# Output bias of the experts: a one-hot product on TensorE, or a scaled row added by POOL

## The chip, the core and the metric

The kernel runs on one core of a Trainium2 chip. The metric is the time of one execution on the device, in microseconds (us), the median of several runs. The core's engines work side by side, each in the order of its own program, and meet at semaphores: TensorE (PE) multiplies matrices and writes PSUM, VectorE (DVE), ScalarE (ACT) and GpSimd (POOL) work on elements, SyncE (SP) starts loads and stores. DVE and ACT read PSUM and SBUF, POOL reads SBUF alone. POOL also issues the gathers and scatters by index.

## The reference

A decoder layer on four sequences of 512 tokens of 512 numbers, all in float32: self-attention, attention to a short memory, and a mixture of experts. The change is in the experts, of which the reference is:

```python
logits = h @ router_weight.T + router_bias
top_vals, top_idx = jax.lax.top_k(logits, TOP_K)          # 2 of 8
top_w = jax.nn.softmax(top_vals, axis=-1)
scores = jnp.zeros_like(logits).at[jnp.arange(T)[:, None], top_idx].set(top_w)
...
expert_out = jnp.einsum('eti,eih->eth', act, down_proj) + down_proj_bias[:, None, :]
out = jnp.einsum('te,eth->th', scores, expert_out)
```

Each token goes to two experts. An expert's output is `act @ down_proj` plus a bias row of that expert, `down_proj_bias[e]`, and the sum is multiplied by the token's share of that expert, `scores[t, e]`.

## The kernel before

**Stages.** The first 1055 us are the self-attention. From there to about 1175 the kernel attends to the memory, normalises, routes, and sorts the tokens by expert into tiles of 256 (`TILE`): 23 tiles (`NT`), the first eight for experts 0 to 7, the other fifteen given out by a table that is computed on the chip. From about 1175 to 1610 runs the expert loop, tile after tile; then the sums are copied to the output.

**One tile.** A tile `tau` has four units `u = 4 tau + ib`, one for each 128 of the 512 hidden numbers of the expert. A float32 product is made of three passes (`PASSES`): an operand is split into a high part, which ACT copies, and a low part, the rest, which DVE subtracts (`dve_lo`, L410). A unit goes round the engines like this:

- SP loads the unit's weights, `gu_raw` (512 KB, `sp_gu`, L1229) and `dn_raw` (256 KB, `sp_dn`, L1238), each into the place of the unit four before, once DVE has made the low part of that one. All these loads stand in one queue, in order.
- PE multiplies the gathered rows with the first weights (`pe_gu`, L1347: 24 products, two units ahead of the rest) into a PSUM bank.
- DVE makes `gate` and `up` of it (L1381, L1383: one input in PSUM, a bias column), then `gu_lo` for three units later (L410), then, after ACT's `sig`, the products `sig` and `up` (L1388, L1390), `dn_lo` and `act_lo` (L410).
- ACT makes `sig` (L1402), `gu_hi` for four units later, `act_hi` and `dn_hi` for the next unit (L306).
- PE multiplies `act` with the second weights (`pe_dn`, L1368: three products of 128x512 for each half tile of 128 tokens), adding up over the four units in one PSUM bank per half tile.

**Once per tile.** At the end of unit 3 PE transposes the rows of the tile after the next (`pe_rows`, L1318); ACT and DVE split them in unit 2 of the tile that follows (`act_rows`, `dve_rows`), and DVE takes the tokens' shares of the expert from the gathered rows (`dve_shares`, L1300 and L1304: `sh`, one number per token). In unit 1 of the next tile ACT reads the finished bank of each half, multiplies it with `sh` and writes `y`, which lies in `ctx_raw` (`act_y`, L1420; semaphore `ys_done`). POOL waits for both halves and for the landing of the scatters before, and then issues two scatters that add `y` to the sums in memory (`pool_y`, L1266). Behind these on POOL stand the two gathers of rows for three tiles later (`pool_rows`, L1254).

**The bias before.** The eight bias rows are loaded once (L1438) into `down_raw`, which POOL has filled with zeros (L1608); ACT and DVE split them into a high part in partitions 0 to 7 and a low part in 32 to 39 of `down_bias` (L1521, L1581). `expert_hot` has a column per tile, 1 in the two partitions of the tile's expert (L977, L1178, from `expert_row`). The first product of each half tile's bank is this column, spread over 128 tokens, with `down_bias` (L1366, 128x512); the other products add to it. So the bias is in the bank when ACT scales it.

**Order.** Each engine's order is the program's, at the end of `decoder_layer` (L1424 to L1642). On ACT a unit is `sig`, `gu_hi`, `act_hi`, `dn_hi`, then what comes once per tile. On SP a step is `sp_gu(u)`, `sp_dn(u - 3)`. On POOL a step is `pool_rows(tau + 2)`, `pool_y(tau)`.

Of the kernel before, what the change touches and what calls it, by code (L numbers as in the profile page):

```python
# [15 lines left out]
F32 = mybir.dt.float32  # L16
F32R = mybir.dt.float32r
# [82 lines left out]
def decoder_layer(nc, x, ctx, ctx_cols, mem_mask, wqkv, wo_rows, router_cols, router_b, gu_w, gu_b, down_w, down_b,  # L100
                  cos_t, sin_t, causal_t, ident_t, iota_t, out):
    stack = ExitStack()
    with stack:
# [701 lines left out]
        empty = st("empty", [P, 2 * NT])  # L805
        expert_row = st("expert_row", [P, 1])
        before_me = st("before_me", [P, P], BF16)
# [28 lines left out]
        bias_add = st("bias_add", [P, IB, 2])  # L836
        down_raw = st("down_raw", [P, D])
        down_bias = st("down_bias", [P, D], F32R)
        expert_hot = st("expert_hot", [P, NT], F32R)
        idx = st("idx", [P, 2 * NT], U32)  # L840
# [11 lines left out]
        for pre in ("m_", "h_"):  # L852
# [5 lines left out]
                   "const_done", "diff_done", "gexp_done", "gate_step", "sel_done", "share_done",  # L858
                   "rank_mm", "down_in", "down_hi", "down_lo", "row_done", "lane_done", "slots_mm", "slots_done", "hot_first", "hot_done", "idx_mm", "empty_done", "idx_done", "place_done", "pos_done", "h_in0", "h_in1", "h_in2", "h_in3", "share_in", "acc_in",
                   "count_mm", "table", "table_done",  # L860
# [3 lines left out]
                   "ah_done", "al_done", "dn_mm", "y_first", "ys_done", "y_add", "out_done"]  # L864
        CONSTS = 16
        z = {name: sem("z_" + name) for name in names2}
# [88 lines left out]
        def pe_idx_first(pe):  # L955

            pe.wait_ge(z["hot_first"], 3)
            pe.wait_ge(z["slots_done"], 1)
            nc.tensor.matmul(SLOTS[:, IDX_AT:IDX_AT + 2 * E], slots[:, :], row_hot[:, 0:2 * E], start=True, stop=True).then_inc(z["idx_mm"], 1)

        def pe_idx_rest(pe):

            pe.wait_ge(z["hot_done"], 2)
            nc.tensor.matmul(LATE_IDX[:, 0:2 * NX], slots[:, :], row_hot[:, 2 * E:2 * NT], start=True, stop=True).then_inc(z["idx_mm"], 1)
# [5 lines left out]
        def dve_first_tiles(dve):  # L970

            dve.wait_ge(z["const_done"], CONSTS - 1)
            nc.vector.tensor_tensor(tile_hot[:, 0:E, :], e_iota[:, :].unsqueeze(1).to_broadcast([P, E, E + 1]),
                                    t_iota[:, 0:E].unsqueeze(2).to_broadcast([P, E, E + 1]), ALU.is_equal).then_inc(z["hot_first"], 1)
            nc.vector.tensor_scalar(row_hot[:, 0:2 * E], first_row[:, :, :].rearrange("p e h -> p (e h)"), row_iota[:, 0:1], None,
                                    ALU.is_equal).then_inc(z["hot_first"], 1)
            nc.vector.tensor_scalar(expert_hot[:, 0:E], t_iota[:, 0:E], expert_row[:, 0:1], None, ALU.is_equal).then_inc(z["hot_first"], 1)  # L977

# [161 lines left out]
        def dve_table(dve):  # L1140
# [6 lines left out]
            def then(ins):  # L1147
# [29 lines left out]
                                    ALU.is_equal).then_inc(z["hot_done"], 1)  # L1177
            nc.vector.tensor_scalar(expert_hot[:, E:NT], tile_e[:, :], expert_row[:, 0:1], None, ALU.is_equal).then_inc(z["hot_done"], 1)  # L1178

# [172 lines left out]
        def pe_dn(pe, u):  # L1352
# [4 lines left out]
            pe.wait_ge(z["dn_lo_done"], u + 1)  # L1357
            if u == 0:
                pe.wait_ge(z["down_lo"], 1)
            for h in range(2):  # L1360
                n = 2 * tau + h
                if ib == 0:
                    if n == 2:
                        pe.wait_ge(z["idx_done"], 2)
                    wait(pe, z["ys_done"], n - 2)
                    nc.tensor.matmul(Y_BANK[n % 3][:, :], expert_hot[:, tau:tau + 1].to_broadcast([P, P]), down_bias[:, :], start=True, stop=False)  # L1366
                for sp_, mp in PASSES:
                    last = nc.tensor.matmul(Y_BANK[n % 3][:, :], act_st[sp_][:, w, h * P:(h + 1) * P], dn[mp][:, ib, :],  # L1368
                                            start=False, stop=(ib == IB - 1 and (sp_, mp) == PASSES[-1]))
                if h == 0 and ib == IB - 1:  # L1370
# [33 lines left out]
        def act_hi(act, u):  # L1404
# [3 lines left out]
            act_split(act_st[0][:, w, :], up[:, w, :], z["ah_done"])  # L1408

        def act_y(act, tau):  # L1410

# [12 lines left out]
        with nc.Block() as block:  # L1424

            @block.sync
            def _(sp):
# [7 lines left out]
                sp.dma_start(iota[:, :], iota_t).then_inc(z["small_in"], 16)  # L1435
                sp.wait_ge(z["const_done"], 1)
                for at in (0, 32):
                    sp.dma_start(down_raw[at:at + E, :], down_b).then_inc(z["down_in"], 16)  # L1438

# [64 lines left out]
            def _(act):  # L1504
                for k in range(ROUNDS):
# [11 lines left out]
                    if k == TOP_AT + IB + 1:  # L1517
                        act_dn_hi(act, 0)
                    if k == H_AT:
                        act.wait_ge(z["down_in"], 32)  # L1520
                        act_split(down_bias[:, :], down_raw[:, :], z["down_hi"])  # L1521
                act_slots(act)
                act_rows(act, 0)
                for u in range(NU):
# [9 lines left out]
                    if ib == 1 and tau:  # L1534
                        act_y(act, tau - 1)
                act_y(act, NT - 1)

            @block.vector
            def _(dve):
                for k in range(ROUNDS):  # L1540
# [37 lines left out]
                    on(lambda t: dve_m_inv(dve, t), k, EXP_AT)  # L1578
                    if k == TOP_AT:
                        dve.wait_ge(z["down_hi"], 1)  # L1580
                        nc.vector.tensor_tensor(down_bias[32:2 * 32, :], down_raw[32:2 * 32, :], down_bias[32:2 * 32, :].bitcast(F32),  # L1581
                                                ALU.subtract).then_inc(z["down_lo"], 1)
# [4 lines left out]
                dve.wait_ge(z["hot_first"], 3)  # L1587
                dve_shares(dve, 0)
# [18 lines left out]
            def _(pool):  # L1607
                nc.gpsimd.memset(down_raw[:, :], 0.0).then_inc(z["const_done"], 1)  # L1608
                for view, steps, base, by_row in ((tok_id[:, :], [[P, TT]], 1, 1), (e_start[:, :], [[T, E + 1]], 0, 0), (e_rows[:, :], [[T // P, E + 1]], TILE // P, 0),
                                                   (first_row[:, :, :], [[T // P, E], [1, TILE // P]], 0, 0),  # L1610
                                                   (e_iota[:, :], [[1, E + 1]], 0, 0), (t_iota[:, :], [[1, NT]], 0, 0), (k_tile[:, :], [[TILE, E - 1]], TILE, 0),
                                                   (row_iota[:, :], [[0, 1]], 0, 1), (lane_iota[:, :], [[1, P]], 0, 0),
                                                   (empty_id[:, :, :], [[0, NT], [P, 2]], T + 1, 1), (expert_row[:, :], [[0, 1]], 0, 1)):
                    nc.gpsimd.iota(view, steps, base=base, channel_multiplier=by_row,
                                   allow_small_or_imprecise_dtypes=True).then_inc(z["const_done"], 1)
                pool.wait_ge(z["const_done"], 12)
                nc.gpsimd.tensor_scalar(expert_row[32:2 * 32, :], expert_row[32:2 * 32, :], -32.0, None, ALU.add).then_inc(z["const_done"], 1)
                pool.wait_ge(z["const_done"], 13)
                nc.gpsimd.memset(ones[:, :], 1.0).then_inc(z["const_done"], 1)
                pool.wait_ge(z["const_done"], 14)  # L1620
                nc.gpsimd.affine_select(before_me[:, :], ones[:, :], [[1, P]], ALU.is_gt, 0.0, base=0, channel_multiplier=-1).then_inc(z["const_done"], 1)
# [76 lines left out]
```

## Time and profile before

| | us |
|---|---|
| median of 3 runs | 1630.09 (1629.74 to 1633.28) |
| the profiled execution | 1634.84 |
| its span, first to last instruction | 1633.0 |
| PE busy | 1489.3 (91%) |
| DVE busy | 1374.6 (84%) |
| ACT busy | 1057.3 (65%) |
| POOL busy | 841.3 (52%) |

The profile is of one execution, which took a little longer than the median. Busy times are sums over stages of different kinds. Matmuls overlap each other, so a full PE isn't PE at its peak rate. A view of the profile names an operation by its line and its output and input tiles; a helper's line (L306 for ACT's copies, L410 for DVE's low parts) stands for many steps, which the tile names tell apart.

### The profile page before, as it was taken

The numbers are of one execution on the slowest core, as the hardware profiler recorded it, in microseconds if no ns is written. First come the engines' busy times: TensorE is split into PE (matmuls) and PEld (weight loads), VectorE is DVE, ScalarE is ACT, GpSimd is POOL, SyncE is SP. The second block draws the span as 40 slices with busy tenths as digits, with TensorE's granted clock in tenths as the row PEclk, the third lists the DMA queues.
The fourth block names the chain that finished last, engine by engine and source line by source line (L and its number), as shares of the span: only waits on it lengthen the run. The fifth ranks groups of instructions, "written<-read, shape, count | busy, mean of one in ns | idle before, by whom it ended". The sixth has DMA issues, their size and how long they took to land. (4 is left out here: it accounts for less than half of the span.)

```text
span 1633.0 us, 31154 instructions
## 1 busy us (share of the span) xinstructions
PE 1489.3 (91%) x8952; PEld 1313.6 (80%) x8952; DVE 1374.6 (84%) x3583; ACT 1057.3 (65%) x2464; POOL 841.3 (52%) x1024
## 2 busy tenths in 40 slices
PE   5789999999999899999999999688699999999994
PEld 4678888888888778888878878578589999999993
DVE  7788898898898788889889889578689988998892
ACT  3677777777777677777777777343146666666661
POOL 7657657657657466656656755267312223222321
PEclk9799999999999999999999999966599999999997
DMA  4000000000000000000000000141458778877775
GB/s 175 1 14 20 2 14 21 1 14 21 1 14 20 3 14 20 1 15 21 1 15 1 1 1 1 32 146 74 142 146 243 234 228 221 225 228 218 198 178 135
DMA packets 62030, 124.95 MB, mean 77 GB/s; under 512 B 20942, under 2 KB 21070, under 8 KB 61792
## 3 DMA queue, kind: packets, MB, share of 16 engines
q1 hardware_dynamic: 51408, 102.24, 19.5%
q0 software_dynamic: 10304, 20.59, 6.5%
q8 instruction: 77, 1.26, 0.3%
q14 instruction: 97, 0.79, 0.2%
q10 hardware_dynamic: 144, 0.07, 0.0%
HBM read 106.08 MB, written 24.71 MB: 80 GB/s over the span
## 5 line engine op out<-in xcount | busy, mean ns | idle before, releaser
L313 ACT ACTIVATE probs<-probs,neg_max 128x512 f32<-128x512 f32 (+3 forms) x512 | 281.7, 552 | 46.4 <-DVE neg_max L422 44.1
L546 POOL TENSOR_SCALAR probs<-probs,row_inv 128x512 f32<-128x512 f32 (+3 forms) x512 | 263.8, 534 | 42.8 <-DVE row_inv L429 42.8
L537 POOL TENSOR_TENSOR rot<-rot,sin 128x512 f32<-128x512 f32 (+1 forms) x96 | 123.8, 1289 | 308.0 <-DVE rot L441 303.7
L218 PE MATMUL bank<-ident,probs 128*128 128x128 f32 x1280 | 186.0, 276 | 59.6 <-DVE pt_lo L410 50.0
L410 DVE TENSOR_TENSOR pt_lo<-bank,pt_hi 128x512 fp32r<-128x512 f32 (+1 forms) x384 | 216.2, 590 | 26.5 <-ACT pt_hi L306 26.4
L306 ACT ACTIVATE pt_hi<-bank 128x512 fp32r<-128x512 f32 (+1 forms) x384 | 186.2, 518 | 74.3 <-PE bank L218 66.2
L422 DVE CUSTOM_DVE_ANT_0 probs<-bank,causal 128x512 f32<-128x512 f32 (+3 forms) x512 | 219.6, 481 | 10.9 <-issue 3.6
L1266 POOL DMA_INDIRECT acc<-ctx_raw,idx x46 | 75.5, 1642 | 297.2 <-ACT ctx_raw L1420 283.0
L218 PEld LDWEIGHTS bank<-ident,probs 128*128 128x128 f32 x1280 | 151.1, 142 | 94.9 <-DVE pt_lo L410 54.7
L1347 PE MATMUL bank<-xt_hi,gu_hi 128*128 128x256 f32 x736 | 209.0, 284 | 3.5 <-issue 2.0
L1347 PE MATMUL bank<-xt_hi,gu_lo 128*128 128x256 f32 x736 | 207.2, 282 | 0.0
L1347 PE MATMUL bank<-xt_lo,gu_hi 128*128 128x256 f32 x736 | 207.2, 281 | 0.0
L208 PE MATMUL bank<-k_hi,q_st 128*128 128x256 f32 (+2 forms) x512 | 173.0, 349 | 2.5 <-DVE xn_lo L410 2.5
L235 PE MATMUL bank<-pt_hi,v_st 128*128 128x256 f32 (+2 forms) x512 | 172.5, 348 | 1.6 <-DVE pt_lo L410 1.6
L208 PE MATMUL bank<-k_lo,q_st 128*128 128x256 f32 (+2 forms) x512 | 157.4, 329 | 0.0
L235 PE MATMUL bank<-pt_lo,v_st 128*128 128x256 f32 (+2 forms) x512 | 156.8, 328 | 0.0
L185 PE MATMUL bank<-xn_hi,w_hi 128*128 128x512 f32 x384 | 153.6, 400 | 0.2 <-DVE rot L441 0.2
L185 PE MATMUL bank<-xn_lo,w_hi 128*128 128x512 f32 x384 | 151.9, 396 | 0.0
L185 PE MATMUL bank<-xn_hi,w_lo 128*128 128x512 f32 x384 | 151.6, 395 | 0.0
L1347 PEld LDWEIGHTS bank<-xt_hi,gu_hi 128*128 128x128 f32 x736 | 139.9, 190 | 7.5 <-issue 4.2
L1347 PEld LDWEIGHTS bank<-xt_lo,gu_hi 128*128 128x128 f32 x736 | 140.2, 190 | 3.0
L1347 PEld LDWEIGHTS bank<-xt_hi,gu_lo 128*128 128x128 f32 x736 | 139.9, 190 | 0.0
(204 smaller groups left out, 3915.0 us busy)
## 6 DMA issues: line engine op xcount, KB each, us to landing
gu_raw<-in_gate_up SPq DMA_DIRECT2D x92, 512.0 KB, 4.3
dn_raw<-in_down SPq DMA_DIRECT2D x92, 256.0 KB, 3.7
w_raw<-in_wqkv SPq DMA_DIRECT2D x8, 768.0 KB, 4.2
w_raw<-in_wo_rows SPq DMA_DIRECT2D x8, 512.0 KB, 3.5
h_rows<-ln_h SPq DMA_DIRECT2D x16, 256.0 KB, 2.0
acc<-x_res SPq DMA_DIRECT2D x4, 1024.0 KB, 5.0
x_res<-in_x SPq DMA_DIRECT2D x3, 1024.0 KB, 11.1
ctx_raw<-in_ctx SPq DMA_DIRECT2D x2, 512.0 KB, 6.9
```

The costliest lines, as they stand in the source:

```text
L185: last = nc.tensor.matmul(PJ_BANK[:, :], w1[sp][:, c, r * P:(r + 1) * P], xn[mp][:, c, b * L:(b + 1) * L], start=first, stop=(c == DC - 1 ...
L208: last = nc.tensor.matmul(S_BANK[k][:, at:at + cols], q_st[:, h, i * P:(i + 1) * P], kk[:, kb, 0:cols], start=(a == 0), stop=(a == 1))
L218: last = nc.tensor.transpose(T_BANK[u % 2][:, k * P:(k + 1) * P], probs[:, hb, P_AT[i] + j * P:P_AT[i] + (j + 1) * P], ident[:, :])
L235: last = nc.tensor.matmul(dst, v_st[:, vb, j, :], rhs, start=(j == 0 and a == 0), stop=(j == QB - 1 and a == 1))
L306: nc.scalar.activation(dst, src, ACT.Copy).then_inc(sem_, 1)
L313: nc.scalar.activation(row, row, ACT.Exp, bias=neg_max[:, hb, i:i + 1], scale=-1.0, accum_out=row_sum[:, hb, i:i + 1]).then_inc(s["exp_don ...
L410: nc.vector.tensor_tensor(dst, src, hi.bitcast(F32), ALU.subtract).then_inc(sem_, 1)
L422: nc.vector.tensor_tensor_reduce(out=probs[:, hb, P_AT[i]:P_AT[i] + (i + 1) * P], in0=S_BANK[k][:, at:at + (i + 1) * P], in1=causal[:, (QB ...
L537: nc.gpsimd.tensor_tensor(rot[0:rows, :], rot[0:rows, :], sin[0:rows, :], ALU.mult).then_inc(s["rot_sin"], 1)
L546: nc.gpsimd.tensor_scalar(row, row, row_inv[:, hb, i:i + 1], 0.0, ALU.mult, ALU.add).then_inc(s["pnorm_done"], 1)
L1266: nc.gpsimd.indirect_dma_start(out=acc, out_offset=bass.IndirectOffsetOnAxis(ap=idx[:, 2 * tau + h:2 * tau + h + 1], axis=0), in_=y[:, 2 * ...
L1347: last = nc.tensor.matmul(GU_BANK[u % 3][:, side * TILE:(side + 1) * TILE], gu[sp_][:, ib, c, side, :], xts[mp][:, k, c, :], start=first, ...
```

## The change

The one-hot product goes, and with it `expert_row`, `expert_hot`, `down_raw`, the split of the bias and the fill with zeros. The first of the other products now starts each bank. Per tile SP loads the expert's bias row to all 128 partitions (256 KB, two buffers), behind the tile's first `dn_raw`. ACT multiplies it with `sh` for each half tile into `y_b` (`act_bias`), behind the last unit's `dn_hi`. POOL adds `y_b` to `y`, one sum of 128x512 for each half as soon as ACT has written it, and waits for both sums ahead of its scatters. The wait of DVE for the use of `sh` three tiles before now asks for POOL's sums instead of ACT's `y`.

```diff
         def sp_dn(sp, e, u):
-            ib = u % IB
+            tau, ib = divmod(u, IB)
             wait(sp, z["dn_lo_done"], u - IB + 1)
             sp.dma_start(dn_raw[:, ib, :], down_w.rearrange("e i h -> (e i) h")[bass.ds(e * I + ib * P, P), :]).then_inc(z[f"dn_in{ib}"], 16)
+            if ib == 0:
+                wait(sp, z["b_scaled"], 2 * (tau - 1))
+                sp.dma_start(down_bias[:, tau % 2, :], down_b[bass.ds(e, 1), :].partition_broadcast(P)).then_inc(z[f"d_in{tau % 2}"], 16)
...
         def pool_y(pool, tau):
...
-            pool.wait_ge(z["ys_done"], 2 * tau + 2)
+            for h in range(2):
+                pool.wait_ge(z["ys_done"], 2 * tau + h + 1)
+                pool.wait_ge(z["b_scaled"], 2 * tau + h + 1)
+                nc.gpsimd.tensor_tensor(y[:, 2 * k + h, :], y[:, 2 * k + h, :], y_b[:, 2 * k + h, :], ALU.add).then_inc(z["y_bias"], 1)
+            pool.wait_ge(z["y_bias"], 2 * tau + 2)
             wait(pool, z["y_add"], 32 * tau)
...
         def dve_shares(dve, tau):
...
-            wait(dve, z["ys_done"], 2 * (tau - 2))
+            wait(dve, z["y_bias"], 2 * (tau - 2))
...
         def pe_dn(pe, u):
...
-            if u == 0:
-                pe.wait_ge(z["down_lo"], 1)
...
                     wait(pe, z["ys_done"], n - 2)
-                    nc.tensor.matmul(Y_BANK[n % 3][:, :], expert_hot[:, tau:tau + 1].to_broadcast([P, P]), down_bias[:, :], start=True, stop=False)
                 for sp_, mp in PASSES:
                     last = nc.tensor.matmul(Y_BANK[n % 3][:, :], act_st[sp_][:, w, h * P:(h + 1) * P], dn[mp][:, ib, :],
-                                            start=False, stop=(ib == IB - 1 and (sp_, mp) == PASSES[-1]))
+                                            start=(ib == 0 and (sp_, mp) == PASSES[0]), stop=(ib == IB - 1 and (sp_, mp) == PASSES[-1]))
...
+        def act_bias(act, tau):
+
+            k = tau % 2
+            act.wait_ge(z["sh_done"], tau + 1)
+            act.wait_ge(z[f"d_in{k}"], 16 * (tau // 2 + 1))
+            wait(act, z["y_bias"], 2 * (tau - 1))
+            for h in range(2):
+                nc.scalar.activation(y_b[:, 2 * k + h, :], down_bias[:, k, :], ACT.Copy, scale=sh[:, tau % 3, h:h + 1]).then_inc(z["b_scaled"], 1)
...
                     if ib == 1 and tau:
                         act_y(act, tau - 1)
+                    if ib == 3:
+                        act_bias(act, tau)
...
-                nc.gpsimd.memset(down_raw[:, :], 0.0).then_inc(z["const_done"], 1)
```

Left out are the other lines of the old bias (L977, L1178, L1436 to L1438, L1519 to L1521, L1579 to L1582, L1617), the new buffers `down_bias` (two rows) and `y_b` (four half tiles), and the counts of the semaphores that follow from them.

## Rows read from the trace of the kernel before

**Rows 1.** Windows of 18 us: busy time by engine, granted clock, DMA share, GB/s

```profile
core 0: us, PE busy (x) PEld busy (x) DVE busy (x) ACT busy (x) POOL busy (x), PEclk, DMA share, GB/s
1403.00:1421.00 18.00, 18.00 (x131) 16.75 (x130) 16.12 (x34) 11.39 (x20) 5.14 (x4) 1.00 0.85 235
```

**Rows 2.** Chain that ended last, from 1140 on by line, and pieces: start, us, what

```profile
by line: PE bank L1347 49.9%; PE bank L1368 24.0%; PE bank L1318 4.3%; issue 2.9%; PE bank L1366 2.0%; POOL at_lane L1130 1.3%; DMA acc<-ctx_raw,idx 1.0%; DVE gu_lo L410 0.9%; PE bank L951 0.8%; DMA xg<-h_rows,idx 0.7%; POOL acc L1266 0.6%;
...
1195.54 0.50 PE bank L1366
...
1214.96 0.87 PE bank L1318 x8
...
1218.65 0.23 PE bank L1366
...
1579.20 0.87 PE bank L1318 x8
```

**Rows 3.** Waits from 1240 to 1560: engine, for whom, us, times, longest

```profile
DVE gate L1381 <- PE bank L1347: 20.2, 17, 1.2
```

**Rows 4.** Timeline of ACT: start, us, line, operation, [idle before, and for whom]

```profile
1417.34 0.62 ACT L306 ACTIVATE dn_hi<-dn_raw 128x512 fp32r<-128x512 f32 x1
1417.86 1.25 ACT L1420 ACTIVATE ctx_raw<-bank,sh 128x512 f32<-128x512 f32 x2
...
1427.97 0.62 ACT L306 ACTIVATE dn_hi<-dn_raw 128x512 fp32r<-128x512 f32 x1
1429.18 0.42 ACT L1402 ACTIVATE sig<-gate 128x256 f32<-128x256 f32 x1 [0.59 <-DVE gate L1381]
```

**Rows 5.** Timeline of DVE in the same tile

```profile
1417.50 0.42 DVE L410 TENSOR_TENSOR act_lo<-up,act_hi 128x256 fp32r<-128x256 f32 x1
1419.04 0.48 DVE L1381 TENSOR_SCALAR gate<-bank,bias 128x256 f32<-128x256 f32 x1 [1.13 <-PE bank L1347]
1419.44 0.47 DVE L1383 TENSOR_SCALAR up<-bank,bias 128x256 f32<-128x256 f32 x1
1419.84 1.22 DVE L410 TENSOR_TENSOR gu_lo<-gu_raw,gu_hi 128x1024 fp32r<-128x1024 f32 x1
1420.97 0.42 DVE L1388 TENSOR_TENSOR sig<-sig,gate 128x256 f32<-128x256 f32 x1
```

**Rows 6.** DMA issues: operation, count, KB each, median us to landing

```profile
gu_raw<-in_gate_up SPq DMA_DIRECT2D x92, 512.0 KB, 4.3
...
xg<-h_rows,idx POOLq DMA_INDIRECT x46, 5.1
```

**Rows 7.** Timelines of POOL and DVE, where both have two SBUF inputs; lines (ns min/median/max)

```profile
1134.16 1.27 POOL L1222 TENSOR_TENSOR gu_lo<-gu_raw,gu_hi 128x512 fp32r<-128x512 f32 x1
...
1134.31 1.15 DVE L1085 TENSOR_TENSOR g_w<-g_w,g_exp 128x4 f32<-128x4 f32 x1
...
L1085 DVE TENSOR_TENSOR g_w<-g_w,g_exp x4: 145/158/1146, 1107.9 to 1167.4; 128x4 f32<-128x4 f32 x4
...
43.76 1.62 POOL L539 TENSOR_TENSOR rope<-rope,rot 128x512 f32<-128x512 f32 x1
...
43.58 0.68 DVE L447 TENSOR_TENSOR q_st<-rope,q_st 64x512 fp32r<-64x512 f32 x1
44.27 1.66 DVE L448 TENSOR_TENSOR q_st<-rope,q_st 64x512 fp32r<-64x512 f32 x1
...
L448 DVE TENSOR_TENSOR q_st<-rope,q_st x64: 685/687/1655, 44.3 to 1016.6; 64x512 fp32r<-64x512 f32 x64
...
L475 DVE TENSOR_TENSOR o_f<-bank,v_and_o x128: 669/683/685, 73.6 to 1046.2; 64x512 f32<-64x512 f32 x128
```

**Rows 8.** Timeline of POOL in the tile of rows 4 and 5

```profile
1419.57 1.63 POOL L1266 DMA_INDIRECT acc<-ctx_raw,idx  x1 [12.01 <-ACT ctx_raw L1420]
...
1424.98 1.04 POOL L1254 DMA_INDIRECT xg<-h_rows,idx  x1 [0.30 <-issue]
```

**Rows 9.** Chain that ended last, in the routing stage

```profile
1086.37 0.68 DVE down_bias L1581
```

**Rows 10.** Timelines of ACT and POOL at the end of the expert loop

```profile
1608.95 1.30 ACT L1420 ACTIVATE ctx_raw<-bank,sh 128x512 f32<-128x512 f32 x2 [1.64 <-PE bank L1368]
...
1611.27 1.57 POOL L1266 DMA_INDIRECT acc<-ctx_raw,idx  x1 [3.87 <-DMA acc<-ctx_raw,idx]
```

More of the change, by code:

```diff
@@ L805, in decoder_layer @@
         empty = st("empty", [P, 2 * NT])
-        expert_row = st("expert_row", [P, 1])
         before_me = st("before_me", [P, P], BF16)
@@ L836, in decoder_layer @@
         bias_add = st("bias_add", [P, IB, 2])
-        down_raw = st("down_raw", [P, D])
-        down_bias = st("down_bias", [P, D], F32R)
-        expert_hot = st("expert_hot", [P, NT], F32R)
+        down_bias = st("down_bias", [P, 2, D])
+        y_b = st("y_b", [P, 4, D])
         idx = st("idx", [P, 2 * NT], U32)
@@ L858, in decoder_layer @@
                    "const_done", "diff_done", "gexp_done", "gate_step", "sel_done", "share_done",
-                   "rank_mm", "down_in", "down_hi", "down_lo", "row_done", "lane_done", "slots_mm", "slots_done", "hot_first", "hot_done", "idx_mm", "empty_done", "idx_done", "place_done", "pos_done", "h_in0", "h_in1", "h_in2", "h_in3", "share_in", "acc_in",
+                   "rank_mm", "d_in0", "d_in1", "b_scaled", "y_bias", "row_done", "lane_done", "slots_mm", "slots_done", "hot_first", "hot_done", "idx_mm", "empty_done", "idx_done", "place_done", "pos_done", "h_in0", "h_in1", "h_in2", "h_in3", "share_in", "acc_in",
                    "count_mm", "table", "table_done",
@@ L864, in decoder_layer @@
                    "ah_done", "al_done", "dn_mm", "y_first", "ys_done", "y_add", "out_done"]
-        CONSTS = 16
+        CONSTS = 13
         z = {name: sem("z_" + name) for name in names2}
@@ L955, in pe_idx_first @@
         def pe_idx_first(pe):
-            pe.wait_ge(z["hot_first"], 3)
+            pe.wait_ge(z["hot_first"], 2)
             pe.wait_ge(z["slots_done"], 1)
@@ L961, in pe_idx_rest @@
         def pe_idx_rest(pe):
-            pe.wait_ge(z["hot_done"], 2)
+            pe.wait_ge(z["hot_done"], 1)
             nc.tensor.matmul(LATE_IDX[:, 0:2 * NX], slots[:, :], row_hot[:, 2 * E:2 * NT], start=True, stop=True).then_inc(z["idx_mm"], 1)
@@ L1177, in dve_table @@
                                     ALU.is_equal).then_inc(z["hot_done"], 1)
-            nc.vector.tensor_scalar(expert_hot[:, E:NT], tile_e[:, :], expert_row[:, 0:1], None, ALU.is_equal).then_inc(z["hot_done"], 1)
         def dve_at(dve, t):
@@ L1435, in _ @@
                 sp.dma_start(iota[:, :], iota_t).then_inc(z["small_in"], 16)
-                sp.wait_ge(z["const_done"], 1)
-                for at in (0, 32):
-                    sp.dma_start(down_raw[at:at + E, :], down_b).then_inc(z["down_in"], 16)
                 for u in range(IB):
@@ L1518, in _ @@
                         act_dn_hi(act, 0)
-                    if k == H_AT:
-                        act.wait_ge(z["down_in"], 32)
-                        act_split(down_bias[:, :], down_raw[:, :], z["down_hi"])
                 act_slots(act)
@@ L1578, in _ @@
                     on(lambda t: dve_m_inv(dve, t), k, EXP_AT)
[L1579 to L1582, printed above, removed]
                 dve_idx(dve, 1, 0, 2 * E, SLOTS[:, IDX_AT:IDX_AT + 2 * E])
@@ L1586, in _ @@
                 dve_rows(dve, 0)
-                dve.wait_ge(z["hot_first"], 3)
+                dve.wait_ge(z["hot_first"], 2)
                 dve_shares(dve, 0)
@@ L1612, in _ @@
                                                    (row_iota[:, :], [[0, 1]], 0, 1), (lane_iota[:, :], [[1, P]], 0, 0),
-                                                   (empty_id[:, :, :], [[0, NT], [P, 2]], T + 1, 1), (expert_row[:, :], [[0, 1]], 0, 1)):
+                                                   (empty_id[:, :, :], [[0, NT], [P, 2]], T + 1, 1)):
                     nc.gpsimd.iota(view, steps, base=base, channel_multiplier=by_row,
                                    allow_small_or_imprecise_dtypes=True).then_inc(z["const_done"], 1)
-                pool.wait_ge(z["const_done"], 12)
-                nc.gpsimd.tensor_scalar(expert_row[32:2 * 32, :], expert_row[32:2 * 32, :], -32.0, None, ALU.add).then_inc(z["const_done"], 1)
-                pool.wait_ge(z["const_done"], 13)
                 nc.gpsimd.memset(ones[:, :], 1.0).then_inc(z["const_done"], 1)
-                pool.wait_ge(z["const_done"], 14)
+                pool.wait_ge(z["const_done"], 11)
                 nc.gpsimd.affine_select(before_me[:, :], ones[:, :], [[1, P]], ALU.is_gt, 0.0, base=0, channel_multiplier=-1).then_inc(z["const_done"], 1)
```

1 line of the change is left out of this document (removed).

## The prediction

> **What bounds the kernel now.** I read the windows first, then the chain that ended last, then the waits, then one tile engine by engine. In the windows of the expert loop TensorE is busy for all of its 18.00 us at a granted clock of 1.00, and VectorE (DVE) for 16.12 of them [rows 1]: one engine is full and the next is close behind. The chain says the same: from 1214.96 to 1579.20 it is TensorE alone, 20 tiles apart, so a tile takes 364.24 / 20 = 18.21 us [rows 2]. How close DVE is, the waits tell: in 320 us of this loop its `gate` step waited 17 times for TensorE, 20.2 us together [rows 3], 1.19 us per tile. Left alone, DVE would need 18.21 - 1.19 = 17.02 us per tile. So taking work from TensorE can win at most 1.19 us per tile before DVE becomes the pace, and anything that holds DVE up by more than that loses.
>
> **The change, part by part.**
>
> TensorE loses two one-hot products per tile. On the chain one takes 0.23 us (the first 0.50), and all of them are 2.0% of its 493 us, 9.9 us [rows 2]. TensorE's tile falls to 18.21 - 0.47 = 17.74 us.
>
> ACT gains two scalings of 128x512 per tile, behind the `dn_hi` copy of the last quarter, ahead of the next `sig`. A copy of that shape took 0.62 us [rows 4]. They start near 1428.5 and end near 1429.7, so `sig`, at 1429.18, moves by some 0.5 us. DVE doesn't want it until its `gu_lo` is over: from the start of `gate` to that of the `sig` product are 1.93 us (1419.04 to 1420.97) [rows 5], of which `gate` and `sig` themselves need 0.48 + 0.42, so 1.03 are spare. Cost: 0. Without that cover, 0.5 us per tile, 11 in all. The scalings wait for a bias that SyncE asked for more than a tile earlier and for POOL's sums of two tiles before, and DVE's `sh` step for those of three before: all long done.
>
> SyncE gains one 256 KB load per tile, between two weight loads; queued behind it, and behind its wait for the scalings of two tiles before, are all later weights. That wait is over when its turn comes: the `dn_lo` that SyncE waits for just ahead of it follows, on DVE, a `sig` that ACT runs behind those scalings. A 512 KB load lands after a median 4.3 us [rows 6], and a bias is used 1.75 tiles after its turn comes. In bytes it is 0.25 MB on top of about 4.2 MB per tile (235 GB/s for 18 us), at a DMA share of 0.85 [rows 1]: some 0.05 more. Reading one row 128 times isn't in the trace; between 0 and one more 512 KB load, 4.3 us, it stays inside its cover. I take 0.
>
> POOL gains two sums of 128x512 per tile, and these I expect to decide. Three questions: what one costs, whom it stops, and where it falls.
>
> One costs 1.27 us: that is what POOL took for a two-input operation of this shape [rows 7].
>
> Whom it stops is shown by two places of the trace [rows 7]. At 1134.16 POOL begins such an operation; DVE's `g_w`, 4 elements from two SBUF inputs, begins 0.15 later and takes 1.15 us, where the shortest took 0.145. It was held for 1.00 us, to 1.15 us after POOL began. At 43.58 DVE runs `q_st` (two SBUF inputs) and POOL's operation takes 1.62: it waited 0.35 us for DVE, got in ahead of DVE's next operation, and that took 1.66 where 0.685 is normal, so DVE was let in at 45.24, 1.13 us after POOL at 44.11. So each waits for the other's whole operation, by turns, 1.13 to 1.15 us for DVE per sum. DVE operations with one input in PSUM don't take part: 128 of `o_f`, spread over the stage in which `q_st` was held so, took 0.669 to 0.685 us [rows 7]. In the expert loop `gate` and `up` read PSUM; `gu_lo`, the two products, `dn_lo` and `act_lo` have both inputs in SBUF.
>
> The Trainium skill (SBUF — State Buffer, "Who interferes with whom") has this as an exclusive lock held for the full instruction, the second one blocked until the first finishes. By it a sum would stop DVE for its full 1.27 us, where the rows give 1.13; the sum below would be 21 x 2 x 0.14 = 5.9 us higher.
>
> Where it falls: take the tile at 1417.50 [rows 4, 5]. If DVE did not wait for TensorE, `gate` would follow `act_lo` at 1417.84 (operations in a row overlap by 0.08, as `gate` and `up` do), `up` at 1418.24, `gu_lo` at 1418.64. ACT writes the first half tile of y from 1417.86 to about 1418.53 and the second to 1419.11. The first sum starts at 1418.53 at the earliest, and at the latest 0.46 later, the lag of today's scatter behind y [rows 4, 8]. If it is ahead of `gu_lo`, it holds that to about 1419.74, 1.10 late; `gu_lo` takes 1.13; the second sum then goes ahead of the `sig` product and holds it 1.13. Together 2.2 us. If `gu_lo` is first, the first sum holds the `sig` product for 1.13 and the second the next product for about 1.0: 2.1 us. Bounds: 0, if both sums fall where DVE reads PSUM or stands, and 2 x 1.27 = 2.54. I take 2.2, since no idle time of DVE is left to hide them once it is the pace.
>
> DVE's tile is then 17.02 + 2.2 = 19.22 us against TensorE's 17.74: DVE paces, and a tile takes 1.01 us more than 18.21. Sums fall in tiles 1 to 22; in the last, DVE has other gaps. 21 x 1.01 = +21.2 us.
>
> What is queued behind the sums on POOL: today's two scatters and then two gathers. Scatters start at 1419.57, the last gather is issued at 1424.98 and lands 5.1 us later [rows 6, 8], near 1430.1; TensorE transposes these rows at 1214.96 + 12 x 18.21 = 1433.5. With the sums the scatter starts near 1422.0 + 0.1 + 0.46 = 1422.6, 3.0 later, and the slack of 3.4 is nearly used up, in a tile that is 1.0 longer. A gather late by less than about 1 us makes `gate` wait just where the first sum would have held DVE, so it adds nothing. Cost 0; more under the rivals.
>
> The start: the fill, an index step and a shift on POOL, two small loads, a split on ACT and three small steps on DVE go. Only DVE's `down_bias`, 0.68 us, lies on the chain [rows 9]; the rest ends ahead of something that waits for a load or for TensorE. Between 0 and -0.7; I take -0.7, because the chain goes right through it.
>
> The end: y's last half is ready at 1608.95 + 1.30 = 1610.25, and its scatter starts at 1611.27, held by the landing of the scatter before [rows 10]. With two sums, 1609.6 + 2 x 1.27 + 0.46 = 1612.6 at the least, +1.4; by way of the scatter before, later by its own two sums less the 0.6 that the first half is ready sooner, +2.0. I take +1.8.
>
> Sum: 21.2 - 0.7 + 1.8 = +22.3 us against the profiled execution's 1634.84 us (span 1633.0). That one is 4.75 above the median of 1630.09; I add the difference to the median: **1652 us**.
>
> **Rivals.**
> *Faster, TensorE stays the pace.* It takes DVE being held less than 17.74 - 17.02 = 0.72 us per tile by the two sums in the stretch from `gate` to the second product. For it: 0.8 us of `gate` and `up` read PSUM, and today's 1.19 us wait stands right there, so the first sum could pass almost unseen, and perhaps the second between two short operations. Against it: the sums are 2.5 us together and follow each other at once, and the free stretch, today some 2 us, shrinks as TensorE gets faster. Price: -9.9 - 0.7 + 1.8 = -8.8, 1621 us. The sign turns at about 1.14 us per tile (21 x (1.14 - 1.19) = -1.1).
> *One sum collides, the other doesn't.* DVE is held 1.13: its tile is 18.15, -0.06 x 21 - 0.7 + 1.8 = about 0: 1630 us. For and against as above.
> *The port is held to POOL's recorded end, or the gather is late as well.* The first gives +5.9: 1658 us; a mechanism of this kernel's two sums, against which the two rows of 1.13 and 1.15 speak. For the second, a gather that lands 3 us later than the median of 5.1 is 3.0 + 3 - 3.4 - 1.0 = 1.6 late, of which about 1 adds nothing: 0.6 us, 13 if it were so in each tile, 6 in every other one.
> *The load is the trouble.* A broadcast that took much longer than 4.3 us would starve the weights behind it; the cover named above and DVE's own pace speak against it. Weights late by 0.5 us per tile give 1652 + 22 x 0.5 = 1663 us.
>
> **How the numbers follow.** The forecast gets 0.57, a range of its own of 1645 to 1656; held port or late gather 0.17; one collision 0.11; TensorE still the pace 0.11; the load 0.04. About 0.2%, 3.3 us, is what a measurement of this kernel can tell from no change. Faster: 0.11 and a little of the one-collision case, 0.13. Same: 0.08. Slower: the rest, 0.79. The range takes in the forecast, the held port and about half of the one-collision case: 1630 to 1661.
>
> **What would show it.** In the new profile: a tile of about 19.2 us between transposes; `gate` hardly waiting for TensorE and TensorE waiting for `act_lo` or `gu_lo`; the longest `gu_lo`, `sig` and `up` products about 1.1 us over today's; POOL's sums at 1.27 us or longer, up to 2.4. Wrong would be: those DVE operations at today's lengths and a tile near 17.8; `sig` delaying DVE; weights or gathered rows landing late.

## The result, and the profile after

The kernel after takes **1654.01 us** (median of 4 runs, 1652.31 to 1654.94), the kernel before, run beside it, 1629.91 (1628.69 to 1633.28): a ratio of 1.0138, 95% interval 1.0118 to 1.0157, so 24.1 us slower. 1652 was predicted, with a range of 1630 to 1661. The profiled execution took 1654.94 us, its span 1652.4.

Where the 19.3 us between the two spans lie can be read from one step that comes once per tile, `gate` of unit 2. Here it is in tiles 1 and 21, before and then after:

```profile
1218.69 0.48 DVE L1381 TENSOR_SCALAR gate<-bank,bias 128x256 f32<-128x256 f32 x1 [1.36 <-PE bank L1347]
1582.94 0.48 DVE L1381 TENSOR_SCALAR gate<-bank,bias 128x256 f32<-128x256 f32 x1 [1.24 <-PE bank L1347]
...
1213.21 0.48 DVE L1381 TENSOR_SCALAR gate<-bank,bias 128x256 f32<-128x256 f32 x1 [1.36 <-PE bank L1350]
1598.76 0.48 DVE L1381 TENSOR_SCALAR gate<-bank,bias 128x256 f32<-128x256 f32 x1 [1.11 <-PE bank L1350]
```

It moves by 364.25 us before and 385.55 after: +21.30 in 20 tiles, 18.21 us per tile against 19.28. From the last `gate` to the end of the span it is 28.02 and 30.99 us, +2.97, and the last tile adds 0.53. The loop began 5.53 us earlier in the profiled execution of after; but among all the profiled executions below it begins between 1181.6 and 1190.4 us with and without the change, so no part of that can be put down to the change. Without it the three terms are 24.8 us, close to the 24.1 between the medians.

So the forecast time came true, and so did its largest term. The tile did not get there in the way the prediction said. The window of 18 us that answers to [rows 1]:

```profile
1403.00:1421.00 18.00, 16.81 (x121) 15.56 (x120) 16.11 (x33) 11.31 (x21) 9.18 (x6) 1.00 0.81 221
```

Two of the waits from 1240 to 1560, the second of which answers to [rows 3]:

```profile
PEld bank L1350 <- issue: 22.8, 16, 1.6
DVE gate L1381 <- PE bank L1350: 21.5, 16, 2.6
```

TensorE is no longer full (16.81 of 18.00), but DVE isn't either: its 16.11 us are what they were, and `gate` still waits for TensorE, 21.5 us in 16 times. TensorE's wait (22.8 us in 16 times) has no releaser in the profile ("issue"); what it waits for is worked out below. Each of the two engines stands idle once per tile. That is no engine at its limit; it is a loop that runs through both. DVE's timeline in one tile answers to [rows 5]:

```profile
1406.20 0.48 DVE L1381 TENSOR_SCALAR gate<-bank,bias 128x256 f32<-128x256 f32 x1 [1.14 <-PE bank L1350]
1406.60 0.47 DVE L1383 TENSOR_SCALAR up<-bank,bias 128x256 f32<-128x256 f32 x1
1406.99 1.21 DVE L410 TENSOR_TENSOR gu_lo<-gu_raw,gu_hi 128x1024 fp32r<-128x1024 f32 x1
1408.12 1.51 DVE L1388 TENSOR_TENSOR sig<-sig,gate 128x256 f32<-128x256 f32 x1
...
1410.62 0.42 DVE L410 TENSOR_TENSOR act_lo<-up,act_hi 128x256 fp32r<-128x256 f32 x1
1411.58 1.29 DVE L410 TENSOR_TENSOR xt_lo<-bank,xt_hi 128x512 fp32r<-128x512 f32 x2 [0.55 <-ACT xt_hi L306]
```

POOL's timeline in the same tile answers to [rows 8]:

```profile
1405.75 3.60 POOL L1265 TENSOR_TENSOR ctx_raw<-ctx_raw,y_b 128x512 f32<-128x512 f32 x2 [9.01 <-ACT ctx_raw L1429]
1409.82 1.79 POOL L1269 DMA_INDIRECT acc<-ctx_raw,idx  x1 [0.47 <-POOL ctx_raw L1265]
```

The first sum (1405.75, about 1.29 us) runs through the end of DVE's wait and through `gate` and `up`, which read PSUM. It is over when `gu_lo` begins, and `gu_lo` takes its usual 1.21. The second sum then waits for `gu_lo` (the two take 3.60 us instead of 2.54), gets in ahead of the `sig` product, and holds that to 1.51 us where it takes 0.42. One sum in two holds DVE, by 1.10 us. In 16 of the 23 tiles it is the `sig` product of unit 2 that is held, in five others `gu_lo`.

TensorE's chain in the same stretch (start, us, what) shows who is late for it:

```profile
1411.79 1.19 issue
1412.97 3.09 PE bank L1350 x24
1416.06 1.40 PE bank L1368 x6
1417.46 2.85 PE bank L1350 x24
1420.31 1.39 PE bank L1368 x6
1421.70 0.87 PE bank L1321 x8
1422.58 2.85 PE bank L1350 x24
```

The group at 1412.97 is the first of the next tile, and by the program `pe_gu` waits there for `xt_lo`, the split of that tile's rows. DVE's `xt_lo` ends at 1411.58 + 1.29 = 1412.87, 0.10 earlier; the lag is 0.10 in every tile from the second on, where it is about 0.31 in most tiles before, with no idle time of TensorE in front of the group. `xt_lo` in turn waits 0.55 us for ACT:

```profile
1410.13 0.42 ACT L306 ACTIVATE act_hi<-up 128x256 fp32r<-128x256 f32 x1 [2.05 <-DVE up L1390]
1410.45 0.62 ACT L306 ACTIVATE dn_hi<-dn_raw 128x512 fp32r<-128x512 f32 x1
1410.97 1.06 ACT L306 ACTIVATE xt_hi<-bank 128x512 fp32r<-128x512 f32 x2
```

ACT's `xt_hi` stands behind `act_hi`, which waits for DVE's `up` product, and behind `dn_hi`, which nothing else on the loop needs; no run moves `dn_hi`.

So the loop is: `gate` of unit 2 at 1406.20; the `sig` and `up` products on DVE, ACT's three copies and `xt_lo` on DVE, to 1412.87 (6.67 us); six groups on TensorE from 1412.97 to 1425.43 (12.46); and there the next `gate` of unit 2 can start, 19.25 us after the last one. Without the 1.10 of the second sum the same loop takes 18.15 us. Before, that would lie just under TensorE's own 18.21, where it can't be seen; runs 1 and 12 bear on this. The one-hot products stood in another group of TensorE, unit 0's products with the second weights, and not in these six.

### The profile page after: what moved, and what is told of

The parts are those of the page before. It is cut to its first block and busy times, and to the rows that moved or that the text cites. A ratio compares the mean times of both kernels' runs of the same rounds, so it can differ in the third digit from the quotient of the medians.

```text
span 1652.4 us, 31266 instructions
## 1 busy us (share of the span) xinstructions
PE 1481.7 (90%) x8906; PEld 1301.6 (79%) x8906; DVE 1394.0 (84%) x3580; ACT 1082.2 (65%) x2509; POOL 923.3 (56%) x1067
## 5 line engine op out<-in xcount | busy, mean ns | idle before, releaser
L1265 POOL TENSOR_TENSOR ctx_raw<-ctx_raw,y_b 128x512 f32<-128x512 f32 x46 | 74.6, 1648 | 216.7 <-ACT ctx_raw L1429 216.7
```

The costliest lines, as they stand in the source:

```text
L1265: nc.gpsimd.tensor_tensor(y[:, 2 * k + h, :], y[:, 2 * k + h, :], y_b[:, 2 * k + h, :], ALU.add).then_inc(z["y_bias"], 1)
```

## The experiments

The theory is the loop: a sum costs what it holds of it. Its rivals: DVE (or DVE with its holds) is the pace, as the prediction had it; POOL's longer step makes gathers late; the new loads or scalings cost time. All 12 runs are in one table. "Tile" is the distance of `gate` of unit 2 from tile 1 to tile 21 over 20, "held" what DVE operations on the loop take over their usual time, in most tiles (in run 4, where the rows are out of the loop, what all of DVE's operations do); "end" is from the last `gate` to the end of the span. Ratios are against runs of the kernel before on the same chip in the same session.

| run | tile, us | held, us | end, us | median, us | ratio, 95% interval |
|---|---|---|---|---|---|
| before | 18.21 | 0 | 28.0 | 1629.91 | |
| after | 19.28 | 1.10 | 31.0 | 1654.01 | 1.0138, 1.0118 to 1.0157 |
| 1 no sums | 18.14 | 0 | 29.5 | 1627.95 | 0.9987, 0.9964 to 1.0010 |
| 2 before with sums | 19.26 | 1.10 | 31.3 | 1656.67 | 1.0158, 1.0120 to 1.0195 |
| 3 fills for sums | 18.39 | 0 | 31.3 | 1636.62 | 1.0034, 1.0015 to 1.0052 |
| 4 rows early | 18.86 | 1.24 | 31.6 | 1643.59 | 1.0072, 1.0046 to 1.0097 |
| 5 gathers ahead | 19.25 | 1.10 | 32.6 | 1659.77 | 1.0178, 1.0164 to 1.0192 |
| 6 sums in a window | 18.14 | 0 | 32.9 | 1633.81 | 1.0017, 1.0007 to 1.0028 |
| 7 first sum alone | 18.22 | 0 | 30.9 | 1632.67 | 1.0005, 0.9983 to 1.0028 |
| 8 second sum alone | 18.71 | 0.57 | 31.1 | 1644.65 | 1.0087, 1.0055 to 1.0119 |
| 9 no sums, rows early | 18.19 | 0 | 28.9 | 1628.76 | 0.9985, 0.9968 to 1.0002 |
| 10 apart | 17.81 | 0 | 35.7 | 1631.47 | 0.9999, 0.9989 to 1.0010 |
| 11 apart, early end | 18.08 | 0 | 34.6 | 1632.75 | 1.0005, 0.9988 to 1.0022 |
| 12 before, rows early | 18.27 | 0 | 31.2 | 1635.97 | 1.0015, 0.9997 to 1.0032 |

**1. After without the sums.**

```diff
-                nc.gpsimd.tensor_tensor(y[:, 2 * k + h, :], y[:, 2 * k + h, :], y_b[:, 2 * k + h, :], ALU.add).then_inc(z["y_bias"], 1)
```

The waits for `y_bias` go as well, or become waits for `ys_done` and `b_scaled`.

> The changed kernel without POOL's two sums per tile (so the output lacks the experts' bias); the load, ACT's scalings and every other wait stay. Theory 1 (the sums cost the time, by holding DVE on a loop gate of unit 2, sig product, xt_lo, TensorE's first product of the next tile, gate of unit 2): without a hold the loop takes 6.67 - 1.09 + 12.35 = 17.9 us, TensorE 17.74; a tile of 17.9, 1622 to 1625 us. Theory 2 (the prediction's: DVE's own work plus what holds it is the pace): also 1621 to 1625. Rival (the broadcast load or ACT's scalings cost a part): above 1640.

The tile is 18.14 us, not near TensorE's own; both theories had put it lower, and the time at 1621 to 1625 us. `gate` of unit 2 in DVE's timeline, in tiles 1 and 21:

```profile
1210.92 0.48 DVE L1379 TENSOR_SCALAR gate<-bank,bias 128x256 f32<-128x256 f32 x1 [1.36 <-PE bank L1348]
...
1573.79 0.48 DVE L1379 TENSOR_SCALAR gate<-bank,bias 128x256 f32<-128x256 f32 x1 [1.11 <-PE bank L1348]
```

(1573.79 - 1210.92) / 20 = 18.14, and `gate` still waits 1.11 us. So with the one-hot products gone and nothing in their place the tile is only 0.07 shorter. TensorE has less work and stands for nearly all of the time won. The loads and scalings are still there, so the rival is out: they don't cost the 24 us.

**2. Before with two sums of a tile of zeros.**

```diff
+            for h in range(2):
+                nc.gpsimd.tensor_tensor(y[:, 2 * k + h, :], y[:, 2 * k + h, :], no_bias[:, :], ALU.add).then_inc(z["y_bias"], 1)
```

POOL fills the tile of zeros once, ahead of the loop.

> The kernel before, with its one-hot products, plus two POOL sums per tile of y and a tile of zeros, ahead of the scatters; no load, no scaling. Theory 1: the one-hot products are not on the loop that the held sig product stands on (TensorE passes them between the loop's end and its next start), so the tile is 19.2 us as in the changed kernel, 1651 to 1656 us. If what TensorE does counts in full beside the hold: 9.9 more, about 1664. Rival (load or scalings cost the time): 1630 to 1634.

With its one-hot products still there it is as slow as after (19.26 us per tile, 1.0158 against 1.0138 with overlapping intervals). The group of the `sig` product (ns min/median/max) has the same longest as after:

```profile
L1393 DVE TENSOR_TENSOR sig<-sig,gate x92: 410/419/1523, 1187.7 to 1622.0; 128x256 f32<-128x256 f32 x92
```

The time is 0.7 us over the range expected. The sums alone make the whole loss, and beside them the one-hot products cost nothing.

**3. Fills of unused tiles in place of the sums.**

```diff
-                nc.gpsimd.tensor_tensor(y[:, 2 * k + h, :], y[:, 2 * k + h, :], y_b[:, 2 * k + h, :], ALU.add).then_inc(z["y_bias"], 1)
+                nc.gpsimd.memset((ctx_hi, ctx_lo)[h][:, 0:3, :].bitcast(F32), 0.0).then_inc(z["y_bias"], 1)
```

> The changed kernel with each sum replaced by a POOL fill with zeros of an unused buffer, 128x1536, about 1.3 us, so POOL is busy and its scatters and gathers late just as with the sums, but POOL reads nothing from SBUF (the output lacks the experts' bias). Theories 1 and 2 (two readers of SBUF exclude each other): no hold, DVE's operations at their old lengths, 1622 to 1627 us. Rival (POOL's time itself, or the late gathers behind it, is the cost): 1645 to 1655.

POOL is busy about as long and at the same place, and DVE isn't held. A row of POOL's timeline:

```profile
1397.72 1.38 POOL L1266 MEMSET ctx_lo<- 128x1536 f32 x1
```

And two of DVE's, in the same tile:

```profile
1397.64 1.22 DVE L410 TENSOR_TENSOR gu_lo<-gu_raw,gu_hi 128x1024 fp32r<-128x1024 f32 x1
1398.77 0.42 DVE L1389 TENSOR_TENSOR sig<-sig,gate 128x256 f32<-128x256 f32 x1
```

`gu_lo` runs beside the fill from 1397.72 to 1398.86 and takes its usual 1.22; the `sig` product starts 0.33 before the fill ends and takes its usual 0.42. So POOL's time and its later scatters and gathers are not what costs the greater part of the 24 us. That it is POOL's reading of SBUF fits: the fill reads nothing, and run 6 shows an operation of DVE with an input in PSUM passing beside the sums. The median is still 9.6 us over the range expected. What is left of this run's loss (tiles of 18.2 to 19.2 among others of 18.14) stands with gathered rows that land late (TensorE waits for them 12 times, 7.4 us).

**4. The next tile's rows and shares in unit 1.** On ACT, and in the same way `dve_rows` and `dve_shares` on DVE:

```diff
-                    if ib == 2 and tau + 1 < NT:
+                    if ib == 1 and tau + 1 < NT:
                         act_rows(act, tau + 1)
```

> The changed kernel with the split of the gathered rows (ACT's xt_hi, DVE's xt_lo and shares) in unit 1 instead of unit 2 of the tile before, so ahead of the held sig product; sums as they are. Theory 1: TensorE no longer waits for xt_lo behind the hold; what is left is DVE with 17.0 us and one hold, a tile of 18.1 to 18.4, 1630 to 1638 us. Theory 2: DVE's work and holds are the same wherever xt_lo stands, 19.2 us per tile, 1650 to 1656.

In the right direction, but not clean, and 5.6 us over the range expected. The sums now hold `sh_mul` (1.23 us for 0.17) and a little of `gu_lo` (1.40 for 1.22), and since `y` comes later on ACT, TensorE waits for gathers:

```profile
PEld bank L1321 <- DMA xg<-h_rows,idx: 20.7, 14, 2.4
```

Undisturbed tiles are 18.2 us. DVE's own 17.02 and a hold of 1.06 + 0.18 would be 18.26: with the loop cut, DVE with its holds is near to being the pace, as the prediction had it. This run alone doesn't settle that.

**5. Gathers one step earlier.**

```diff
+                pool_rows(pool, 2)
...
-                    if tau + 2 < NT:
-                        pool_rows(pool, tau + 2)
+                    if tau + 3 < NT:
+                        pool_rows(pool, tau + 3)
```

> The kernel after, with each gather of rows issued one step earlier on POOL (ahead of the sums and scatters of the tile before), sums where they are. Theory (the loop gate, sig product, act_lo, rows, next tile's gu on TensorE sets the tile, and the sum lengthens it by its hold of 1.1 us): nothing gained, a tile of 19.2 us, 1650 to 1656 us. Rival (a good part of the 24 us is gathers that land late behind the sums): tiles near 18.4, 1633 to 1640 us.

Every tile from the second on is 19.25 us, and no gather is late. The late gathers of after are hidden in its loop. The median is 3.8 us over what was expected, the tile is not; the end is 1.6 us later than in after.

**6. The sums wait until DVE reads PSUM.** Run 5, and:

```diff
+            if tau + 2 < NT:
+                pool.wait_ge(z["al_done"], IB * (tau + 1) + 3)
             for h in range(2):
```

> As the run with the gathers ahead, and the two sums of a tile wait for act_lo of unit 2 of the next tile, so that they run beside xt_lo, gate and up of DVE, which read PSUM. Theory (a sum costs only by holding an operation of DVE on the loop that has both inputs in SBUF): sig product of unit 2 back at 0.42 us, sh_mul or gu_lo held off the loop, tile 18.14 to 18.2, 1626 to 1632 us. Rival (the sums cost by taking bandwidth or by holding any operation of DVE): still 19 us and more per tile, over 1645 us.

18.14 us, as without sums. In POOL's timeline of one tile:

```profile
1401.34 2.53 POOL L1267 TENSOR_TENSOR ctx_raw<-ctx_raw,y_b 128x512 f32<-128x512 f32 x2 [8.69 <-DVE act_lo L410]
```

In DVE's:

```profile
1401.81 1.29 DVE L410 TENSOR_TENSOR xt_lo<-bank,xt_hi 128x512 fp32r<-128x512 f32 x2 [0.55 <-ACT xt_hi L306]
1403.01 0.90 DVE L1305 TENSOR_TENSOR sh_mul<-xg,tile_hot 128x16 f32<-128x16 f32 x1
```

The two sums stand beside `xt_lo`, which has an input in PSUM and takes what it always does. `sh_mul` is held by 0.73 us in 21 tiles, and that costs nothing: it is behind `xt_lo`, off the loop. The expected 1626 to 1632 us were missed by 1.8, at the end (32.9 us against 28.0).

**7 and 8. One sum of the two.** Run 7; in run 8 it is `tau + 2` in the waits and `2 * k + 1` in the sum:

```diff
-            for h in range(2):
-                pool.wait_ge(z["ys_done"], 2 * tau + h + 1)
-                pool.wait_ge(z["b_scaled"], 2 * tau + h + 1)
-                nc.gpsimd.tensor_tensor(y[:, 2 * k + h, :], y[:, 2 * k + h, :], y_b[:, 2 * k + h, :], ALU.add).then_inc(z["y_bias"], 1)
+            pool.wait_ge(z["ys_done"], 2 * tau + 1)
+            pool.wait_ge(z["b_scaled"], 2 * tau + 1)
+            nc.gpsimd.tensor_tensor(y[:, 2 * k + 0, :], y[:, 2 * k + 0, :], y_b[:, 2 * k + 0, :], ALU.add).then_inc(z["y_bias"], 2)
...
```

Left out are waits for `ys_done` and `b_scaled` of both halves, ahead of the scatters and on DVE.

> The kernel after with the first of a tile's two sums alone (the second half tile goes out without the experts' output bias). Theory (the first sum falls into DVE's wait ahead of gate of unit 2): no operation of DVE held in most tiles, a tile of 18.15 to 18.3 us, 1626 to 1633 us. Rival (each sum holds DVE by 1.1 us): a tile of 19.2 us, over 1648 us.

> The kernel after with the second sum alone (the first half tile goes out without the experts' output bias). It begins as soon as the second half of y is there, about when gate of unit 2 ends, and so may be done before gu_lo or hold it. Theory (only the share of a sum that holds an operation on the loop counts): gu_lo of unit 2 held by what is left of the sum when up ends, 0.5 to 1.1 us, and the tile longer by just that, 18.6 to 19.25 us, 1636 to 1655 us. Rival (it takes both sums): no hold, 18.15 us, 1626 to 1632 us.

The first alone holds nothing; 18 of 20 tiles are 18.12 to 18.17, and in the other two TensorE waits for gathered rows. The second alone holds `gu_lo` by what is left of it when `up` ends. POOL's timeline in run 8:

```profile
1402.38 1.30 POOL L1264 TENSOR_TENSOR ctx_raw<-ctx_raw,y_b 128x512 f32<-128x512 f32 x1 [9.66 <-ACT ctx_raw L1432]
```

DVE's in the same tile:

```profile
1402.17 0.48 DVE L1384 TENSOR_SCALAR gate<-bank,bias 128x256 f32<-128x256 f32 x1 [1.11 <-PE bank L1353]
1402.57 0.47 DVE L1386 TENSOR_SCALAR up<-bank,bias 128x256 f32<-128x256 f32 x1
1402.96 1.80 DVE L410 TENSOR_TENSOR gu_lo<-gu_raw,gu_hi 128x1024 fp32r<-128x1024 f32 x1
```

1.80 for 1.22: held by 0.58, and the tile is 18.71 = 18.14 + 0.57. With 0, 0.57 and 1.10 held the tile is 18.14 (18 tiles of run 7), 18.71 (run 8) and 19.25 (run 5): what is held on the loop comes out in full.

**9. No sums, and the rows in unit 1** (shares stay in unit 2). Run 1, with `ib == 1` for `act_rows` and `dve_rows`.

> The kernel after without POOL's sums (the experts' output bias is left out of the result) and with the split of the next tile's rows in unit 1 instead of unit 2 on ACT and DVE; the shares stay in unit 2. Theory (without sums the loop of 5.58 + 12.56 = 18.14 us hides what TensorE saved): with the loop cut the removed one-hot products show, a tile of 17.7 to 17.85 us, 1617 to 1622 us. Rival (TensorE's saving is lost to DVE's own pace or to slower matmuls, wherever the rows stand): a tile of 18.1, 1626 to 1630 us.

Ten of its tiles are 17.80 to 17.92 us, where run 1 has none under 18.13; the other ten are 18.1 to 19.2, and TensorE waits nine times for gathered rows, 8.2 us together. TensorE's saving is there once the loop is cut, but late gathers take it back, and the expected 1617 to 1622 us were missed.

**10. Apart.** The whole kernel after; rows in unit 1, gathers two steps earlier, and the sums a tile later:

```diff
+                pool_rows(pool, 2)
+                pool_rows(pool, 3)
...
-                    if tau + 2 < NT:
-                        pool_rows(pool, tau + 2)
+                    if tau + 4 < NT:
+                        pool_rows(pool, tau + 4)
...
+            if tau + 3 < NT:
+                pool.wait_ge(z["al_done"], IB * (tau + 2) + 2)
             for h in range(2):
```

DVE's `sh` step waits for ACT's `ys_done` and `b_scaled` in place of `y_bias`, so that it doesn't stand behind the later sums.

> The kernel after, whole, in three moves: rows split in unit 1 instead of unit 2; gathers issued two steps earlier; the two sums of a tile wait for act_lo of unit 1 of the tile after next, so that they run beside xt_lo, gate and up. Theory (the loop is cut, and sums stand beside operations that read PSUM): gu_lo held by 0.5 us at most, a tile of 17.75 to 17.9 us, 1618 to 1625 us, faster than both kernels. Rival (DVE with the sums is the pace wherever they fall): 18.5 us and more per tile, over 1635 us.

The same window as [rows 1]:

```profile
1403.00:1421.00 18.00, 18.00 (x132) 16.87 (x131) 16.43 (x35) 12.49 (x22) 8.75 (x7) 1.00 0.82 233
```

TensorE is full again, with the bias added by POOL. `gate` of unit 2 in tiles 1 and 21:

```profile
1218.81 0.47 DVE L1384 TENSOR_SCALAR gate<-bank,bias 128x256 f32<-128x256 f32 x1
...
1575.04 0.47 DVE L1384 TENSOR_SCALAR gate<-bank,bias 128x256 f32<-128x256 f32 x1
```

356.23 / 20 = 17.81 us, 0.40 under before. That is TensorE's own tile: four groups of 2.84, four of 1.40 and the transposes' 0.87 are 17.83. But 20 x 0.40 = 8 us are given back behind the loop: from the last `gate` to the end are 35.7 us, 7.7 more than before, so it takes as long as before and, by the two ratios, 1.4% less than after, not the 1618 to 1625 us expected. POOL's last scatters:

```profile
1597.49 1.82 POOL L1271 DMA_INDIRECT acc<-ctx_raw,idx  x1 [1.31 <-DMA acc<-ctx_raw,idx]
1602.95 1.57 POOL L1271 DMA_INDIRECT acc<-ctx_raw,idx  x1 [3.64 <-issue]
...
1608.36 1.57 POOL L1271 DMA_INDIRECT acc<-ctx_raw,idx  x1 [1.33 <-DMA acc<-ctx_raw,idx]
1613.50 1.56 POOL L1271 DMA_INDIRECT acc<-ctx_raw,idx  x1 [3.57 <-issue]
```

Each pair waits for the pair before it to land, the sums of the last tiles stand on POOL between them, and in both pairs the second scatter starts 3.6 us after the end of the first. Run 12 shows that this last part is not of the sums.

**11. The same, with the last tiles' sums as early as they can be.** `if tau + 5 < NT` in place of `tau + 3`.

> The run with the three moves had tiles of 17.81 us and lost its gain after the loop, where scatters of four tiles stood in a row (from the last gate to the end 35.7 us, 28.0 in the kernel before). The same here, but the sums of the last four tiles start as soon as their y is there. Theory (TensorE's saving shows once the loop is cut and the end is not late): the same 17.81 us per tile up to the last few, the end back to 28 to 30 us behind the last gate, 1621 to 1627 us, faster than before by 0.3 to 0.6%. Rival (the end is late for another reason): 1630 us and more.

17.82 us per tile as far as the switch, but for one of 19.23 at the start; the two tiles at the switch take 20.04 and 19.22 (3.6 us lost), and the end is still 34.6 us. The rival holds: the end is late for more than the waiting sums, and the expected 1621 to 1627 us were missed. The last pair of scatters here has the gap of 3.6 us inside it that run 10 shows, where in the kernel before it has 0.3.

**12. Before, with rows in unit 1 and gathers two steps earlier.**

> The kernel before (with its one-hot products) with the rows split in unit 1 and the gathers two steps earlier, no sums. Theory (in the kernel before TensorE's own work sets the tile at 18.21 us and the loop of 18.14 is hidden below it): no change, a tile of 18.2 us, 1628 to 1633 us. Rival (moving the rows gains by itself, with or without the one-hot products): a tile of 17.8 us, 1621 to 1625 us.

Tiles of 18.15 and 18.26 us by turns, as before, but for one of 19.43 at the start: the loop did not bind there, and moving the rows gains nothing by itself. The median is 3 us over what was expected (end 31.2 us), its interval includes no change. The last pair of scatters:

```profile
1611.76 1.57 POOL L1266 DMA_INDIRECT acc<-ctx_raw,idx  x1 [3.77 <-DMA acc<-ctx_raw,idx]
1616.76 1.56 POOL L1266 DMA_INDIRECT acc<-ctx_raw,idx  x1 [3.43 <-issue]
```

The gap of 3.4 us is here too, without sums, where the kernel before has 0.3, and the end is 3.1 us later. Only runs 5, 6, 10, 11 and 12 have it in the last pair, and these are the five in which the gathers are issued earlier. So some 3 of the 7.7 us that run 10 gives back at its end come with the earlier gathers and not with the sums; what the gap is stays open.

## Why the prediction was right, and where it wasn't

**TensorE's own tile**, 17.74: it is 17.81 (run 10). The two products are worth 0.40 and not 0.47.

**The step that failed**, though the total held, is "DVE's tile is then 17.02 + 2.2 = 19.22 us against TensorE's 17.74: DVE paces". Both of its terms were wrong by some 1.1 us, against each other. The hold is 1.10 per tile and not 2.2, because `gate` goes on waiting for TensorE, and the first sum passes in that wait and beside `gate` and `up`; the prediction had said that no idle time would be left to hide it. And what the hold is added to is not DVE's busy 17.02 but the loop's 18.14. 18.14 + 1.10 = 19.24, 17.02 + 2.2 = 19.22. The total was right by this chance. "1.19 us per tile of waiting" [rows 3] was read as DVE's spare time; runs 1 and 9 show that TensorE's smaller work gains only 0.07 of it while the rows stand in unit 2.

**The rival "one sum collides"** had its condition come true and its price wrong: 1630 us, with a tile of 17.02 + 1.13 = 18.15; by the loop it is 18.14 + 1.10. **The rival "TensorE stays the pace"** is wrong for the same reason: run 1 has no hold at all, and its tile is 18.14 and not 17.74.

**How long a sum holds.** [Rows 7] gave 1.13 to 1.15 us from the sum's start. In run 8 `gu_lo` would have taken 1.22 from 1402.96; it ended at 1404.76, so it was let in at 1403.54, 1.16 us after the sum began at 1402.38 and 0.14 ahead of its recorded end. The Trainium skill (SBUF — State Buffer, "Who interferes with whom") has the lock held for the whole instruction; the rows agree but for that 0.14. The same section of the Trainium skill says that an operation of DVE with two SBUF inputs contends with one of GpSimd that reads SBUF, not with one that only writes it, and run 3 agrees: 0.42 us beside a fill, 1.51 behind a sum.

**ACT, SyncE.** The scalings take longer than the 0.62 us assumed, 0.71, and stay hidden:

```profile
L1417 ACT ACTIVATE y_b<-down_bias,sh x46: 706/708/714, 1203.0 to 1624.2; 128x512 f32<-128x512 f32 x46
```

The bias loads land after 4.6 us, the weights after 4.5 where it was 4.3, and nothing waits for either. Both costs were 0, as said.

**Gathers.** Their median to landing is 5.8 us where it was 5.1. They land late in some tiles, as the rival had it for half of them; run 5 shows that this adds nothing beside the hold, and runs 3 and 9 that it does where there is none.

**The end** was put at +1.8 and is +2.97. It goes by way of the scatter before, as one of the two cases said:

```profile
1626.07 2.90 POOL L1265 TENSOR_TENSOR ctx_raw<-ctx_raw,y_b 128x512 f32<-128x512 f32 x2
1630.34 1.57 POOL L1269 DMA_INDIRECT acc<-ctx_raw,idx  x1 [1.38 <-DMA acc<-ctx_raw,idx]
```

The tile before last's scatter starts 3.75 us after its `y` instead of 1.71 (+2.0, the figure of that case), its `y` starts 0.56 later against the last `gate`, and the rest is small. **The start**, -0.7, is lost in the 9 us by which executions differ there.

## What to carry to other kernels

Two engines that both wait a little in every tile are not two engines with room: look for a loop of waits through both, add up one round of it, and compare that with the fullest engine before pricing what an edit to either gains. In these runs a sum on GpSimd, which reads SBUF, cost as much as it held an operation of VectorE on that loop, in full, and nothing per tile where it stood beside operations with an input in PSUM; so its place mattered more than its length. What a loop gains also has to get through the end of the kernel: here a chain of scatters took all of it back.

## What the runs showed that was not expected

The second of two scatters starts 0.3 us after the end of the first in most tiles, and 3.4 to 6.0 us after it in some pairs at the end (the rows of runs 10 and 12 above); by the program it waits for nothing of its own there. In the traces of all 14 kernels such a pair is the first that has no gathers on POOL between it and the pair before; the pair after that has 0.3 again, and any later one has the gap. So gathers issued earlier leave more such pairs at the end. Why is open. And ACT's scaling from SBUF to SBUF takes 0.71 us, where its copy of the same shape took 0.62 [rows 4].
